# A quantised intermediate turned by a transposing DMA, and a down product moved behind the convolution

## What is computed

```python
xq = int4_quant(x)                       # by the mean of |x| of the row, clipped to -8..7
gate = bitlinear(xq, w_gate, s_gate)     # ternary weights, 512 -> 1376
up = bitlinear(xq, w_up, s_up)
gate = jnp.square(jax.nn.relu(gate))
inter = int8_quant(up * gate)            # by the max of |.| of the row
return bitlinear(inter, w_down, s_down)  # 1376 -> 512
...
x = x + _L0_ffn_ref(_L0_cond_ref(x, ...), ...)
```

## Time and profile before

| what | value |
|---|---|
| median of 3 runs | 241.48 us (241.46 to 244.11) |
| the profiled execution | 242.03 us, of which 240.2 us are the span of its instructions |
| TensorE busy | 82% of the span |
| VectorE busy | 84% |
| ScalarE busy | 52% |
| mean share of the 16 DMA engines used by the SyncE queue | 42.3% |

### The profile page before, as it was taken

How to read it: one execution, slowest core, us unless ns; L and a number is a source line. 1 busy time by engine, 2 the same in 40 slices (tenths; PEclk the granted TensorE clock), 3 DMA queues, 4 the chain that set the end, 5 groups by cost and what they waited for, 6 DMA issues and landing times.

```text
span 240.2 us, 4382 instructions
## 1 busy us (share of the span) xinstructions
PE 196.2 (82%) x1352; PEld 109.0 (45%) x1352; DVE 202.5 (84%) x525; ACT 124.3 (52%) x196; POOL 23.7 (10%) x27
## 2 busy tenths in 40 slices
PE   1001655794979999999999999999999999998873
PEld 1001344562645555555555555555555545553431
DVE  6997999859688978889898988989898988989791
ACT  0095898021768292836547292845638292744710
POOL 6036390044000000000000000000000000000000
PEclk9999996898999999999999999999999999999998
DMA  3799940557013052536254342725353362221303
GB/s 83 282 341 302 328 170 3 164 161 213 0 45 90 0 146 77 147 104 186 59 159 105 113 123 98 201 57 176 74 145 96 122 168 65 72 61 31 87 0 87
DMA packets 17002, 29.67 MB, mean 124 GB/s; under 512 B 2912, under 2 KB 2976, under 8 KB 16992
## 3 DMA queue, kind: packets, MB, share of 16 engines
q1 hardware_dynamic: 16704, 29.55, 42.3%
q0 software_dynamic: 160, 0.00, 0.0%
q10 hardware_dynamic: 128, 0.00, 0.0%
HBM read 25.27 MB, written 4.28 MB: 123 GB/s over the span
## 4 chain that ended last, share of the span: by engine, by line
PE 63%; DVE 17%; DMA 8%; ACT 6%; issue 4%; SPq 1%; ACTq 0%; DVEq 0%
PE gate_ps L540 14%; PE down_ps L580 14%; PE conv_ps L446 13%; PE up_ps L542 13%; DMA raw_gate<-in_L_ffn_w_gate_dram 5%; PE tr_act_ps L436 3%; PE tr_act_ps L556 2%; ACT g L684 2%; DMA toep<-k_back 2%; PE tr_dve_ps L565 2%; DVE inter L1034 1%; DVE inter L887 1%; ACT g L687 1%; PE tr_dve_ps L456 1%; DVE kb L922 1%
## 5 line engine op out<-in xcount | busy, mean ns | idle before, releaser
L540 PE MATMUL gate_ps<-gate_t,q_t 128*128 128x416 bf16 (+2 forms) x192 | 69.4, 362 | 1.9 <-DVE q_t L967 1.7
L542 PE MATMUL up_ps<-up_t,q_t 128*128 128x416 bf16 (+2 forms) x192 | 69.3, 361 | 0.0
L684 ACT ACTIVATE g<-gate_ps,gu_scale 128x416 f32<-128x416 f32 (+2 forms) x48 | 30.6, 638 | 73.3 <-PE up_ps L542 68.6
L1034 DVE SCALAR_TENSOR_TENSOR inter<-up_ps,gu_scale,g 128x416 f32<-128x416 f32 (+2 forms) x48 | 33.3, 695 | 17.7 <-ACT g L687 17.1
L580 PE MATMUL down_ps<-down_t,i_t 128*128 128x512 bf16 (+1 forms) x176 | 40.6, 379 | 0.3 <-DVE o_sb L1088 0.3
L446 PE MATMUL conv_ps<-toep,x_t 128*64 128x512 f32 (+3 forms) x256 | 38.0, 439 | 1.1 <-DMA toep<-k_back 0.9
L1038 DVE TENSOR_REDUCE imax<-inter 128x1 f32<-128x416 f32 (+2 forms) x48 | 30.3, 631 | 1.7
L540 PEld LDWEIGHTS gate_ps<-gate_t,q_t 128*128 128x128 bf16 x192 | 18.9, 98 | 22.9 <-issue 7.8
L687 ACT ACTIVATE g<-g 128x416 f32<-128x416 f32 (+2 forms) x48 | 28.2, 587 | 1.5
L446 PEld LDWEIGHTS conv_ps<-toep,x_t 128*64 128x64 f32 x256 | 17.2, 136 | 20.1 <-issue 15.9
L542 PEld LDWEIGHTS up_ps<-up_t,q_t 128*128 128x128 bf16 x192 | 18.9, 99 | 14.4 <-issue 0.6
(11 more groups left out here) (170 smaller groups left out, 252.4 us busy)
## 6 DMA issues: line engine op xcount, KB each, us to landing
toep<-k_back SPq DMA_DIRECT2D x16, 512.0 KB, 4.0
x_in<-in_x_dram SPq DMA_DIRECT2D x32, 128.0 KB, 2.8
x_res<-in_x_dram SPq DMA_DIRECT2D x32, 128.0 KB, 2.7
out_dram<-o_sb SPq DMA_DIRECT2D x32, 128.0 KB, 2.3
raw_gate<-in_L_ffn_w_gate_dram SPq DMA_DIRECT2D x1, 1536.0 KB, 9.5
raw_up<-in_L_ffn_w_up_dram SPq DMA_DIRECT2D x1, 1536.0 KB, 16.1
raw_down<-in_L_ffn_w_down_dram SPq DMA_DIRECT2D x1, 1536.0 KB, 15.3
raw_down<-in_L_ffn_w_down_dram SPq DMA_DIRECT2D x1, 1216.0 KB, 17.8
```

Source lines behind the costliest of these rows:

```text
L540: pe.matmul(gate_ps[bank][:, 0:cn], q_t[p][:, i, :], gate_t[:, i, c0:c0 + cn], start=(i == 0), stop=(i == KB - 1))
L542: mm = pe.matmul(up_ps[bank][:, 0:cn], q_t[p][:, i, :], up_t[:, i, c0:c0 + cn], start=(i == 0), stop=(i == KB - 1))
L684: nc.scalar.activation(g2[bank][:, 0:cn], gate_ps[bank][:, 0:cn], ACT.Relu, scale=gu_scale[p][:, 0:1]).then_inc(relu_done, 1)
L1034: v.scalar_tensor_tensor(out=inter[:, c0:c0 + cn], in0=up_ps[bank][:, 0:cn], scalar=gu_scale[p][:, 1:2], in1=g2[bank][:, 0:cn], op0=ALU.mu ...
```

## The change

1. The intermediate of tiles 0 to 14 is turned by `dma_start_transpose`, issued by SyncE as the first instruction of body m, once `inter_quant` has counted m. `i_t` becomes two buffers; `inter_q` is padded with zeros to 1408 columns (eleven blocks of 128). TensorE's eleven transposes and the two copies on ScalarE and VectorE go, and so do the waits of `xt` and `qt` on those copies. The last tile (k = 16) is turned as before.
2. VectorE waits for that DMA (`it_loaded`) before it writes the next `inter_q`.
3. `down` stands last in TensorE's body, behind `conv`, where it stood between `xt` and `qt`. On VectorE `y_mask` now stands ahead of `o_sb`.
4. The hardware loop is written out.

```diff
-        inter_q = sb("inter_q", [P, I], BF16)
-        i_t = sb("i_t", [P, IB, P], BF16)
+        inter_q = sb("inter_q", [P, IB * P], BF16)
+        i_t = [sb(f"i_t{p}", [P, IB, P], BF16) for p in range(2)]
...
         def iterations(eng, body, last=T):
-            for m in range(LOOP0):
-                body(m, m // 2, m % 2, m)
-            with eng.Fori(LOOP0 // 2, LOOP1 // 2) as i:
-                for p in range(2):
-                    body(2 * i + p, i, p, None)
-            for m in range(LOOP1, last + 1):
+            for m in range(last + 1):
                 body(m, m // 2, m % 2, m)
...
             def body(m, j, p, k):                       # SyncE
                 n = m + 2
+                if k is None or 1 <= k < T:
+                    sp.wait_ge(inter_quant, m)
+                    wait(sp, down_done, m - 2 if k is None else k - 2)
+                    sp.dma_start_transpose(i_t[1 - p][:], inter_q[:]).then_inc(it_loaded, 16)
                 if k is None or k < T - 2:
                     sp.wait_ge(xt_turned, n - 1)
                     load_x(n, p)
...
             def xt(n, j, p):
-                wait(pe, it_act_copied, n - 2)
...
             def qt(n):
-                wait(pe, it_dve_copied, n - 1)
...
-            def down(m, k):
-                pe.wait_ge(it_act_copied, m)
+            def down(m, p, k):
+                if k == T:
+                    pe.wait_ge(it_act_copied, 1)
+                else:
+                    pe.wait_ge(it_loaded, 16 * m)
...
             def body(m, j, p, k):                       # TensorE
                 if k is None or k < T:
                     products(m, p, 0)
-                if k is None or k >= 1:
-                    turn_inter(m, k)
+                if k == T:
+                    turn_last()
...
-                if k is None or k >= 1:
-                    down(m, k)
                 if k is None or k < T - 1:
                     qt(m + 1)
...
                     conv(m + 2, j + 1, p)
                 if k == 0:
                     turn_down(5)
+                if k is None or k >= 1:
+                    down(m, p, k)
...
-                if k is None or k >= 1:                 # ScalarE, the copy of turned blocks 0 to 5
-                    act.wait_ge(it_turned, 2 * m - 1)
+                if k == T:
+                    act.wait_ge(it_turned, 1)
...
+            v.memset(inter_q[:, I:IB * P], 0.0)
...
-                if k is None or k >= 1:                 # VectorE, the copy of turned blocks 6 to 10
-                    dve.wait_ge(it_turned, 2 * m)
+                if k == T:
+                    dve.wait_ge(it_turned, 2)
...
-                        v.tensor_scalar(inter_q[:], inter[:], ROUND, None, ALU.subtract).then_inc(inter_quant, 1)
+                        if k is None or k >= 1:
+                            dve.wait_ge(it_loaded, 16 * m)
+                        v.tensor_scalar(inter_q[:, 0:I], inter[:], ROUND, None, ALU.subtract).then_inc(inter_quant, 1)
...
+                        dve.wait_ge(it_loaded, 16 * (T - 1))
...
+                if k is None or k < T - 2:
+                    y_mask(m + 2)
                 if k is None or k >= 1:
 
                     dve.wait_ge(down_done, m)
...
-                if k is None or k < T - 2:
-                    y_mask(m + 2)
```

More of the change, by code:

```diff
@@ L225, in adaln_ffn @@
         it_dve_copied = sem("it_dve_copied")
+        it_loaded = sem("it_loaded")
         down_done = sem("down_done")
@@ L544, in products, with turn_last @@
                 mm.then_inc(gu_done, 1)
[L546 to L554, removed]
+            def turn_last():
+                pe.wait_ge(y_masked, T)
+                keep_clock(8)
+                pe.wait_ge(last_quant, 1)
+                pe.wait_ge(xt_copied, T)
                 for c in range(IT_SPLIT):
@@ L558, in turn_inter @@
                 mm.then_inc(it_turned, 1)
-                if k == T:
-                    pe.wait_ge(inter_quant, m)
-                pe.wait_ge(q_copied, m + 1 if k is None else min(k + 1, T))
+                pe.wait_ge(inter_quant, T)
+                pe.wait_ge(q_copied, T)
                 for c in range(IT_SPLIT, IB):
@@ L576, in down @@
                 for c in range(IB):
-                    if c == IT_SPLIT:
-                        pe.wait_ge(it_dve_copied, m)
+                    if c == IT_SPLIT and k == T:
+                        pe.wait_ge(it_dve_copied, 1)
                     r = P if c < IB - 1 else IR
-                    mm = pe.matmul(down_ps[:], i_t[0:r, c, :], down_t[0:r, c, :],
+                    mm = pe.matmul(down_ps[:], i_t[1 - p][0:r, c, :], down_t[0:r, c, :],
                                    start=(c == 0), stop=(c == IB - 1))
@@ L698, in body @@
                     down_copy(0)
-                if k is None or k >= 1:
-                    act.wait_ge(it_turned, 2 * m - 1)
-                    nc.scalar.copy(i_t[:, 0:IT_SPLIT, :].rearrange("p c t -> p (c t)"),
+                if k == T:
+                    act.wait_ge(it_turned, 1)
+                    nc.scalar.copy(i_t[1 - p][:, 0:IT_SPLIT, :].rearrange("p c t -> p (c t)"),
                                    tr_act_ps[:, 0:IT_SPLIT * P // 2].bitcast(BF16)).then_inc(it_act_copied, 1)
@@ L1046, in body @@
                     y_scale(m + 1, 1 - p, step)
-                if k is None or k >= 1:
-                    dve.wait_ge(it_turned, 2 * m)
+                if k == T:
+                    dve.wait_ge(it_turned, 2)
                     nb = IB - 1 - IT_SPLIT
-                    v.tensor_copy(i_t[:, IT_SPLIT:IB - 1, :].rearrange("p c t -> p (c t)"),
+                    v.tensor_copy(i_t[1 - p][:, IT_SPLIT:IB - 1, :].rearrange("p c t -> p (c t)"),
                                   tr_dve_ps[:, 0:nb * P // 2].bitcast(BF16))
-                    v.tensor_copy(i_t[0:IR, IB - 1, :], tr_dve_ps[0:IR, nb * P // 2:(nb + 1) * P // 2].bitcast(BF16)
+                    v.tensor_copy(i_t[1 - p][0:IR, IB - 1, :], tr_dve_ps[0:IR, nb * P // 2:(nb + 1) * P // 2].bitcast(BF16)
                                   ).then_inc(it_dve_copied, 1)
```

## The result

| | before | changed |
|---|---|---|
| median | 241.47 us | 263.77 us (263.55 to 264.46) |
| ratio | | 1.093 (1.089 to 1.097) |
| the profiled execution's span | 240.2 us | 262.4 us |

The changed kernel is 22.3 us slower; the forecast was +20.0.

What follows compares the result with a forecast made beforehand. TensorE was taken to set the pitch, 10.77 us a body. 13 x 12.35 = 160.6 less 139.98 gave +20.6, the ends +0.3 - 0.9, so +20.0: span 260.2, time 261.5 us, range 256 to 300.

Steps and rivals of the forecast that it cites:

- The lost cover: TensorE, down product moved last: waits of about 1.1 us before qt and 0.35 before the convolution; +1.35 us a body.
- Chunk 2's bank: TensorE before chunk 2: it waits until about S+3.7 for the bank gated(0) reads, saving some 0.1 us, not 0.61.
- (c): Gap between transposes of x and qt: y_q and copied x come early enough, not slower, 239.5 or 233 us; chance 0.02.
- (d): The change doesn't do as it says, an earlier wait absorbs the lost cover: about 241.5 us; chance 0.04.
- The transposing DMA: SyncE's queue: delays the loads of x and toep behind it, taken as 3.5 us, giving a pitch of 12.35.
- X: Time by which the transposing DMA delays loads behind it on SyncE's queue, issue and data together; taken as 3.5 us.
- threshold of 3.04: The X in us at which the bound through toep, (21.2+X)/2, equals the pitch of 12.12.
- rival (a): SyncE's queue: the DMA is cheap, X under 3.04, only lost cover counts: +17.0, 258.5 us; chance 0.32.
- +0.23 a body: Pitch of 12.35 at X = 3.5 instead of 12.12, set by late toep loads.
- the loop through `toep`: From one body's intermediate through DMA and toep load to the body after next: two pitches, at least 21.2+X us.
- The loop: Hardware loop written out: costed at nothing, bounds -0.1 and +0.1 us a body.
- The ends: Last bodies: +0.3 us in body 14, -0.9 us in body 15, where chunk 2 ends earlier.

Runs made afterwards that it cites:

- everything but the move of x: Changed kernel with loads ahead of the transposing DMA and the down product back between x and qt, transposes of x left behind chunk 2: 239.60 us, ratio 0.991.
- the unrolled one: The kernel before with only the hardware loop written out: 241.26 us, ratio 1.000, pitch 10.71.
- the repetition: The changed kernel as it is, run once more for a second profile: 266.21 us, one run.

## Why the prediction was right

**The lost cover**, the main term, was right as a mechanism and in size: forecast pitch 12.12 without any late load, measured 12.06 in nine of thirteen bodies, and in all thirteen once the loads were ahead. Moving the down product alone, without the DMA, costs as much as the whole change (264.3 us), but that the two totals agree is chance: there the lost cover is 1.74 us a body, here it is 12.06 - 10.77 = 1.29, and the other 7.7 us are late loads and slow clock. Rivals (c) and (d) are out.

**Chunk 2's bank** was right: 0.45 us of waiting took the place of most of the transposes' 0.61, and the kernel with everything but the move of x has a pitch of 10.70 where the unrolled one has 10.71. Of its 1.7 us against the unrolled kernel, 1.4 lie in the last two bodies of the profiles, where the chain that ends the kernel had waited for those transposes (8.73 and 18.5 us against 9.12 and 19.5).

**The transposing DMA** was right in kind, and its size X was off for most bodies: 3.5 was taken, and 2.5 to 2.9 is what the medians of its rows give. By the prediction's own threshold of 3.04 it doesn't set their pitch, so rival (a) was the truth for them, and the forecast's +0.23 a body isn't there. That the total still fell short by only 2.3 us has another reason, one that the prediction lacked: X lies so near the threshold that some `toep` loads come late (bodies 3, 5 and 7, with X at 3.3 to 3.6), body 1 has none of the slack that the others have (its intermediate comes at 71.77, S+1.5, and `x_in`, issued at 73.31, held the transposes of x by 2.84 us), and two of these waits were followed by a convolution at half clock. Sum of that: 7.7 us where the prediction had 13 x 0.23 = 3.0, and of the 7.7 only 1.55 come by the loop through `toep` that those 3.0 stand for. That the total came out so near is in part luck: with X at 2.5 the same sum would have said +17.0, and in the profiles body 0 gave back 1.3 us that have nothing to do with the change. With two DMAs X is clear of the threshold and the loop over two bodies appears, though as one long body in two.

The page that the prediction weighed (the Trainium skill, VectorE: DVE Perf Modes, The three transpose paths) has 1309 ns for one 128x128 block; eleven blocks here land 3.6 us after one issue, 0.33 us a block with the fixed part in it, so here its figure couldn't be multiplied by the number of blocks.

**The loop** was right at nothing (ratio 1.000). **The ends** were right: +0.1 and -1.0 against +0.3 and -0.9.

## What to carry to other kernels

Before a step is moved on the engine that sets the pitch, ask what becomes ready while it runs: the down product was the cover for two results that came 0.8 and 0.6 us before they were needed, and 0.6 us less work couldn't pay for losing 2.4 us of cover. A DMA that waits for a result and is issued from the same queue as the loads makes those loads wait for that result too: issue the loads first. A saving in front of a wait goes into the wait, until other work is moved into it.

## What was not expected of the hardware

A transposing DMA of 128x1408 bf16 within SBUF took 1.3 to 1.9 us of the issuing queue, mostly 1.4, and landed after 3.6 to 3.8 us. TensorE's granted clock fell to 1.2 GHz during convolutions in bodies with long waits (0.77 + 1.06 us, 2.84 + 0.97 us), and a step of 2.37 us took 4.07; waits of 0.77 and 0.34 us in each body never did this in the profiles with the loads first. It isn't regular: in body 7 of the changed kernel waits of 0.77 and 0.82 us, and in body 3 of the repetition one of 1.54 us right ahead of the convolution, left the clock at full speed. What decides it stays open.
